# Head and fill of an attention block: a load moved to another queue, and one tile's products made early

## The reference

```
h = (h - mu) * rsqrt(var + EPS);  h = h * gamma + beta
q, k, v = w_qkv @ h + b_qkv
attn = softmax(q @ k.T / sqrt(C));  out = w_proj @ (attn @ v) + b_proj
return x + out
```

## Time and profile before

| what | value |
|---|---|
| median of three runs | 123.59 us |
| the profiled execution's own time | 123.28 us |
| its span, first to last instruction | 121.4 us |
| PE busy | 114.4 us, 94% |
| DVE busy | 93.3 us, 77% |
| ACT busy | 92.2 us, 76% |
| POOL busy | 90.0 us, 74% |
| mean granted TensorE clock | 0.983 |

### The profile page before, as it was taken

How to read it: one execution, slowest core, us unless ns; L and a number is a source line. 1 busy time by engine, 2 the same in 40 slices (tenths; PEclk the granted TensorE clock), 3 DMA queues, 4 the chain that set the end, 5 groups by cost and what they waited for, 6 DMA issues and landing times.

```text
span 121.4 us, 3255 instructions
## 1 busy us (share of the span) xinstructions
PE 114.4 (94%) x1213; PEld 81.9 (67%) x1213; DVE 93.3 (77%) x240; ACT 92.2 (76%) x129; POOL 90.0 (74%) x75
## 2 busy tenths in 40 slices
PE   5899979899999999999999999999999999997990
PEld 1254447476678877777677777777677777787990
DVE  4677799999687779997677797775777977775532
ACT  2127589999988888888888887888988888887430
POOL 2045258799999999999959879999658777777300
PEclk9986999999999999999999999999999999999998
DMA  3595004999999999999999899989999999999102
GB/s 109 151 331 188 0 0 86 168 144 212 175 101 205 202 155 210 230 202 148 236 213 196 140 216 158 237 185 213 212 119 236 184 209 143 230 221 137 43 5 86
DMA packets 66624, 20.15 MB, mean 166 GB/s; under 512 B 63408, under 2 KB 65968, under 8 KB 66608
## 3 DMA queue, kind: packets, MB, share of 16 engines
q1 hardware_dynamic: 64304, 18.23, 85.7%
q10 hardware_dynamic: 2304, 1.71, 7.0%
HBM read 2.36 MB, written 2.10 MB: 37 GB/s over the span
## 4 chain that ended last, share of the span: by engine, by line
PE 78%; DMA 8%; DVE 7%; ACT 4%; issue 1%; ACTq 1%; SPq 0%
PE o_ps L809 33%; PE scores L787 10%; PE scores L791 10%; PE scores L788 10%; DMA ptT<-p_hl 4%; DMA beta_c<-in_L_conv_beta_dram 3%; DVE row_max L562 3%; PE scores L848 3%; PE o_ps L837 2%; ACT probs L431 2%; PE misc L757 1%; PE misc L758 1%; PE misc L759 1%; PE misc L767 1%; PE misc L766 1%; PE scores L831 1%
## 5 line engine op out<-in xcount | busy, mean ns | idle before, releaser
L346 POOL TENSOR_TENSOR p_hl<-probs,p_hl 128x1024 f16<-128x1024 f32 x32 | 68.1, 2136 | 10.4 <-ACT p_hl L438 10.4
L562 DVE TENSOR_REDUCE row_max<-scores 128x1 f32<-128x1024 f32 x32 | 39.0, 1220 | 15.2 <-PE scores L791 14.9
L431 ACT ACTIVATE probs<-scores,exp_bias,esc 128x1024 f32<-128x1024 f32 x32 | 38.5, 1203 | 11.5 <-DVE exp_bias L567 11.3
L809 PE MATMUL o_ps<-v_hi,ptT 128*128 128x128 f16 x448 | 42.3, 219 | 0.2 <-DVE out_sb L602 0.2
L809 PEld LDWEIGHTS o_ps<-v_hi,ptT 128*128 128x128 f16 x448 | 35.5, 98 | 3.7 <-issue 0.5
L438 ACT ACTIVATE p_hl<-probs 128x1024 f16<-128x1024 f32 x32 | 33.8, 1057 | 1.0
L809 PE MATMUL o_ps<-v_lo,ptT 128*128 128x128 f16 x224 | 28.0, 219 | 0.0
L787 PE MATMUL scores<-z_hi,t_hi 128*128 128x512 f16 x64 | 24.3, 379 | 1.2 <-ACT probs L431 1.2
L791 PE MATMUL scores<-z_hi,t_lo 128*128 128x512 f16 x64 | 24.3, 379 | 0.0
L788 PE MATMUL scores<-z_lo,t_hi 128*128 128x512 f16 x64 | 24.2, 379 | 0.0
L809 PEld LDWEIGHTS o_ps<-v_lo,ptT 128*128 128x128 f16 x224 | 21.9, 98 | 3.1
(11 more groups left out here) (142 smaller groups left out, 152.9 us busy)
## 6 DMA issues: line engine op xcount, KB each, us to landing
out_dram<-out_sb ACTq DMA_DIRECT2D x13, 128.0 KB, 2.9
x_sb<-in_x_dram SPq DMA_DIRECT2D x3, 512.0 KB, 4.3
ptT<-p_hl SPq DMA_TRANSPOSE x59, 3.7
x_sb<-in_x_dram SPq DMA_DIRECT2D x2, 256.0 KB, 3.2
out_dram<-out_sb SPq DMA_DIRECT2D x1, 192.0 KB, 2.0
wqkv_sb<-in_L_conv_w_qkv_dram SPq DMA_DIRECT2D x1, 128.0 KB, 3.6
out_dram<-out_sb SPq DMA_DIRECT2D x1, 128.0 KB, 1.9
wp_sb<-in_L_conv_w_proj_dram SPq DMA_DIRECT2D x1, 64.0 KB, 3.5
```

Of the source, the lines that this page charges most:

```text
L346: nc.gpsimd.tensor_tensor(p_hl[:, g % RING, 1], probs[:, g % RING], p_hl[:, g % RING, 0], ALU.subtract).then_inc(plo_ready, 1)
L431: nc.scalar.activation(probs[:, g % RING], scores[:, g % SLOTS], ACT.Exp, bias=exp_bias[:, g:g + 1], scale=esc[:], accum_out=row_sum[:, g: ...
L562: nc.vector.tensor_reduce(row_max[:, g:g + 1], scores[:, g % SLOTS], AX_X, ALU.max).then_inc(max_ready, 1)
L809: return nc.tensor.matmul(dst, a, b, start=start, stop=stop)
```

## The change

Five things are changed.

1. ACT issues the load of `x`'s second half, ahead of its three small loads. SP issues only the first half, and each of SP's further loads is issued one place earlier.
2. On DVE, `g_diag` is made after the channel statistics of both halves instead of before them, and the group mean's three small operations (L533, L535, L538) come ahead of the reduction for the largest |gamma| (L609).
3. On PE, the group mean's product comes first, then the product with `g_diag`, then A's product, and only then the product with `bq_c`, which waits for `c_loaded`.
4. The warm-up matmuls are 6 + 2, 1, 3 and 5 instead of 6, 3, 3 and 6.
5. The four `KEEP_WARM` matmuls are gone. In their place stand the eight products of tile 0's high probabilities with `v_hi` (`first_products`), ahead of tile 4's scores; `values(0)` makes the other sixteen.

```
 FIRST_WARM = 6
-SECOND_WARM = 3
+SECOND_WARM = 2
 THIRD_WARM = 3
-WARM_UP = 6
-KEEP_WARM = 4
+WARM_UP = 5
...
 # SP
-            for half in range(2):
-                cols = slice(half * HALF, (half + 1) * HALF)
-                sp.dma_start(x_sb[:, cols], x_d[0, :, cols]).then_inc(x_first[half], 16)
+            sp.dma_start(x_sb[:, 0:HALF], x_d[0, :, 0:HALF]).then_inc(x_first[0], 16)
...
 # ACT
+            act.dma_start(x_sb[:, HALF:N], x_d[0, :, HALF:N]).then_inc(x_first[1], 16)
             act.dma_start(gamma_c[:], col(gamma)).then_inc(gcol_loaded, 16)
...
 # DVE
-            dve.wait_ge(gcol_loaded, 16)
-            nc.vector.tensor_scalar(g_diag[:], ident32[:], gamma_c[:], None, ALU.mult).then_inc(gdiag_ready, 1)
...
             channel_stats(0, 0)
             channel_stats(0, 1)
+            dve.wait_ge(gcol_loaded, 16)
+            nc.vector.tensor_scalar(g_diag[:], ident32[:], gamma_c[:], None, ALU.mult).then_inc(gdiag_ready, 1)
+
+            group_mean(0)
             dve.wait_ge(gmax_psum, 1)
             nc.vector.tensor_reduce(g_max[:, 0:1], scores[:, 1, HALF:HALF + P], AX_X, ALU.max,
                                     apply_absolute_value=True).then_inc(gmax_all, 1)
-            group_mean(0)
...
 # PE
+            def first_products():
+
+                pe.wait_ge(hi_transposed[0], 16)
+                pe.wait_ge(vhi_ready, 2)
+                pe.wait_ge(bo_ready, 1)
+                for k in range(TILES):
+                    nc.tensor.matmul(o_ps[:, 0, 0:P], ptT[:, 0, 0, k], v_hi[:, k * P:(k + 1) * P], start=(k == 0),
+                                     stop=False)
+
             def values(g):
...
                     hi = ptT[:, g % PT_RING, 0, k]
-                    product(hi, v_hi[:, keys], k == 0, False)
+                    if g:
+                        product(hi, v_hi[:, keys], k == 0, False)
                     product(hi, v_lo[:, keys], False, False)
...
                 if g == 3:
                     group_mean(1)
-                    pe.wait_ge(bo_ready, 1)
-                    for _ in range(KEEP_WARM):
-                        nc.tensor.matmul(o_ps[:, 0, 0:HALF], ones16[:], warm[:], start=True, stop=True)
+                    first_products()
                     group_var(1)
```

More of the change, by code:

```diff
@@ L792, in score_tile @@
                 last.then_inc(scores_ready, 1)
+            def first_products():
[5 more added lines that the diff above has]
+                                     stop=False)
             def values(g):
                 b = g // TILES
-                if g < LAST - 1:
+                if g and g < LAST - 1:
                     pe.wait_ge(hi_transposed[g % RING], 16 * (g // RING + 1))
-                else:
+                elif g:
                     pe.wait_ge(hi_moved, g - LAST + 2)
@@ L852, in _ @@
             warm_up(FIRST_WARM)
-            pe.wait_ge(const_dve, 2)
+            warm_up(SECOND_WARM)
+            pe.wait_ge(const_dve, 4)
+            group_mean(0)
             pe.wait_ge(gdiag_ready, 1)
@@ L856, in _ @@
                              ).then_inc(gmax_psum, 1)
-            warm_up(SECOND_WARM)
             pe.wait_ge(wqk_loaded, 16)
+            nc.tensor.matmul(scores[:, 0, 0:P], wqkv_sb[:, 0], wqkv_sb[:, 1], start=True, stop=True
+                             ).then_inc(a_psum, 1)
+            warm_up(1)
             pe.wait_ge(c_loaded, 32)
             nc.tensor.matmul(scores[:, 0, HALF:HALF + 1], wqkv_sb[:, 1], bq_c[:], start=True, stop=False)
[L861 to L864, removed]
             group_var(0)
```

## The result

The changed kernel took 125.66 us (median of four executions, 125.34 to 127.3) against 123.32 for the kernel before beside it. The ratio is 1.0207, 95% interval 1.0162 to 1.0251 (a ratio in this document leaves out the executions that are more than 1.5% above the fastest of their kernel, while a median, a lowest and a highest time are of all executions, so the two can differ). The forecast was 123.3, its range ended at 124.4: it missed, on the slow side.

What follows compares the result with a forecast made beforehand. It took small serial steps to bound the head, ACT, DVE and PE in turn the fill, then PE almost alone. Terms 0 - 0.05 + 0.05 - 0.2 - 0.10 = -0.30 us took the median from 123.59 to 123.3; range 122.2 to 124.4.

Steps and rivals of the forecast that it cites:

- the long middle: From about 30 us on: PE almost alone sets the time, so its gains by then reach the end one for one.
- the warm-up term: PE's head, ahead of the first T product: one of six warm-up matmuls fewer, -0.2 us.
- The loads: Head, x's two halves: both land at about 4.1, second statistics step starts at 4.8, taken as 0 us.
- both late: Rival for the head's loads: both halves land at about 4.7, +0.55, with the rest +0.25: 123.85 us; chance 0.20.
- gamma and beta: Head, ACT's small loads: about 0.45 us later, but hidden by the statistics unless they land after about 6.5.
- The order on DVE and PE: Head: on DVE a later group variance, net +0.05 us; on PE no wait for beta ahead of the group mean, -0.05.
- The fill: Fill up to 30 us: early products shorten `values(0)`, but DVE can move only 0.10; -0.10 us, bounds 0 and -0.23.
- The clock's fall in the fill: Rival: more PE idle time between 21 and 22.7 us brings half clock, with the rest +1.5: 125.1 us; chance 0.08.

Runs made afterwards that it cites:

- a_again: The changed kernel unaltered, run once more: 125.4 us (twelve executions), ratio 1.0046 to the kernel before.
- f_all_long: The changed kernel at full work with five warm-up matmuls instead of two behind the first six: 123.51 us (12 executions), ratio 0.998 to the kernel before.
- f_base_long: The kernel before at full work with five warm-up matmuls instead of three behind the product with `g_diag`: 123.5 us (12 executions), ratio 0.9993.
- b_again: The kernel before unaltered, against itself: 124.69 us (ten executions), ratio 1.0084.
- e3_fill: The kernel before with only the eight early products in place of the four keep-warm matmuls: 124.16 us (ten executions), ratio 1.0039.
- e1_load: The kernel before with only the load of x's second half moved to ACT's queue: 126.24 us (four executions), ratio 1.0255.
- r_base: The kernel before with the low transposes cut to half their size, part of the low correction left out: 122.54 us (12 executions).

## Why the prediction was wrong

**The step that failed first** is in the first part: "So the long middle contains no slack that the change touches. Whatever PE gains by about 30 us arrives at the end, one for one". It rested on PE being busy for 15.00 of 15.00 us from 90 to 105. That is one window, of one execution. The transposes run beside PE at the same rate with next to no reserve, and PE waits for them where they fall behind. In the pair of profiles a lead of 0.43 became a loss of 1.8. The row that would have said so stood in the same window: a DMA share of 1.11. With the transposes cut the middle is 90.4 to 90.8 in all eight profiles, so what full transposes cost is 1.0 us in before and 3.2 in the changed kernel's first profile. That difference is partly a draw: a_again lost 1.9. Whether coming 0.4 us earlier makes such waits likelier isn't settled. The kernels with early products had middles of 93.7, 92.4, 92.4 and 92.3, those without 91.45, 91.5, 91.6, 91.9, 92.4 and 92.7, one profile each, but f_all_long and f_base_long, a dozen executions each, don't differ.

**The second step that failed is the warm-up term**, "one of six is gone ahead of the T product ... I take -0.2". In the profile it was right in size. Across executions the head's filler does something else: with eleven of them ahead of the group mean the clock turned to full before it in all five profiles, with seven to nine in some executions and not in others, in both kernels (b_again and e3_fill have before's head and T products at 12.76 and 12.63). The sum took the clock of one execution as fixed. The prediction named this, "if the clock turns at another time than in the execution shown", but it is none of its rivals, and has no price in the T product and no chance. The price is 1.8 us in the T product (12.70 against 10.89). The new head as a whole costs 123.63 - 122.54 = 1.1 in the median of a dozen executions on one chip; on another it is 122.79 - 122.5 = 0.3, which ten executions don't separate from nothing.

**The loads**: forecast 0 with both landing at about 4.1. They landed about 4.3 and 4.5 (issued at 0.72 and 0.73, 3.6 and 3.8 us to landing), the first 0.9 later than when it was issued ahead of the other, the second 0.2 earlier. The statistics ended at 5.60 for before's 5.54. Right, though the sign of "both late", a first half that lands after 4.2, came true by 0.1: it cost 0.06 and not 0.55, since the second half landed earlier than that rival had it. The Trainium skill's rule on issuing engines ("DMA: Bandwidth & Descriptors", section "Issuing engines are not separate DMA queues"), cited in the prediction, agrees with the trace: the second half's gain of 0.2 is within the 0.44 of the issue delay.

**gamma and beta**: hidden in the full change, as written; not hidden where `g_diag` stays first (e1_load).

**The order on DVE and PE**: forecast +0.05 with bounds 0 and 0.25; measured at a settled clock 5.06 - 4.92 = +0.14. Within its bounds, but nearly three times the size.

**The fill**: forecast -0.10 with products at 21.4, a wait of 0.2 for `v_lo` and DVE's maximum of tile 5 directly behind the scaling of tile 0. All three signs came: the products at 21.23, the wait as 0.2 inside the first eight products of `values(0)`, and the maximum at 26.41 behind the scaling at 26.10. But the gain is twice the forecast: from the first T product to `values(2)` it is 29.95 - 11.59 = 18.36 before and 29.52 - 11.36 = 18.16 after, 0.20, and 0.20 again with a settled clock (0.0 in the median there). The forecast let DVE move only up to the end of the scaling's record, 26.73; in the changed kernel that record ends at 26.50, and the maximum starts 0.09 ahead of its end.

**The clock's fall in the fill** did not happen: the fill ran at full clock in the profile of the change.

How the 1.5 us divide is an estimate and not a measurement: 0.3 to 1.1 from the clock in the head, by the two pairs with cut transposes, and so some 0.4 to 1.2 left for the middle. In the first pair of profiles the whole loss is in the middle. No run shows that the change makes the middle longer, rather than one kernel's draws being longer than the other's. Nor is every wait there one for a transpose: PE's longest in e3_fill is 1.3 us for `out_sb` behind 105 us, and its cause wasn't sought.

## What to carry to other kernels

Before counting a gain in the head one for one, look for every stream that runs beside the busy engine at its rate, queues that only issue included; here halving one of two transposes took 1 to 3 us out of the middle, more than all of the change's terms. Don't take filler matmuls for waste: three more of them took 2 us off the changed kernel with cut transposes. Measure their effect over a dozen executions, since one profile shows one of several heads. A load put ahead of a tiny one on the same queue delayed whoever waited for the tiny one (e1_load, about 1.1 us).

## What the runs showed of the hardware

The column of the granted clock can read 1.00 over a stretch at half rate. From 8 to 12 us of b_again (window: us, busy by engine, clock, DMA share, GB/s) it stands at 1.00, while three warm-ups there took 1.49 us, the time at half clock:

```profile
8.00:12.00 4.00, 4.00 (x13) 1.90 (x14) 2.93 (x11) 2.47 (x6) 2.86 (x7) 1.00 0.67 238
```

```profile
8.28 1.49 PE L848 MATMUL scores<-warm,ones 128*128 128x512 f16 x3
```

In these traces the column shows a later fall and return (0.50 in the windows above); where the clock had never turned, it shows nothing. So a mean of 1.000 belongs to the best executions of r_base (121.44) and to its poorest (123.89), and 0.986 lies between. The time of a known matmul told more here: three warm-ups in 0.81 us or in 1.49.

Some issues of a transpose in before take 2.0 to 2.3 us instead of 1.3, as the one at 100.04 above. From 34 us on six of them come, mostly 10 to 12 us apart. Close to each, one transpose lands 2.5 to 3.4 us behind the one ahead of it, where it is mostly 0.7 to 1.9. They coincide with loads of instructions on another queue (the page counts ten). That is a coincidence in time; no run varied it.
